# Cross attention with another order of one step's turns on TensorE, ScalarE and VectorE, and squares taken from SBUF

## What is computed

```python
kvx = jnp.einsum('bsi,oi->bso', cond, w_kv_x)
kx, vx = jnp.split(kvx, 2, axis=-1)
kx = _ln(kx.reshape(b, sc, g, d), kxln_w, kxln_b)
vx = vx.reshape(b, sc, g, d)
xout = _gqa(qx, kx, vx).reshape(b, s, nh * d)
...
cat = jnp.concatenate([core, xout], axis=-1)
catq = _div_clamp_fp8(cat, proj_smooth)
```

## Time and profile before

| | us |
|---|---|
| median of 3 runs | 2798.78 (2798.61 to 2798.89) |
| the profiled execution | 2799.96 |
| its span | 2798.2 |
| PE busy, share of the span | 2278.0 (81%) |
| DVE | 2104.4 (75%) |
| POOL | 1571.4 (56%) |
| ACT | 1554.5 (56%) |
| DMA queue 1, share of the 16 engines' span | 12.3% |

### The profile page before, as it was taken

How to read it: one execution, slowest core, us unless ns; L and a number is a source line. 1 busy time by engine, 2 the same in 40 slices (tenths; PEclk the granted TensorE clock), 3 DMA queues, 4 the chain that set the end, 5 groups by cost and what they waited for, 6 DMA issues and landing times. The chain is left out here.

```text
span 2798.2 us, 50477 instructions
## 1 busy us (share of the span) xinstructions
PE 2278.0 (81%) x18514; PEld 1812.5 (65%) x18514; DVE 2104.4 (75%) x4502; ACT 1554.5 (56%) x3129; POOL 1571.4 (56%) x1619
## 2 busy tenths in 40 slices
PE   2466662699999999999999999999999999855556
PEld 1243441578877877877877877877877878644334
DVE  8888885477787778778787787778778787558763
ACT  4455451566666666666666666666666667411211
POOL 2465655766766766767666766766767655340000
PEclk8687875999999999999999999999999999977778
DMA  2001103110010010110110111010010100073100
GB/s 105 16 29 40 46 23 115 55 38 31 26 50 32 25 44 34 31 44 32 32 38 31 34 43 32 32 44 26 31 52 25 32 9 1 1 271 96 40 12 8
DMA packets 74482, 119.45 MB, mean 43 GB/s; under 512 B 21168, under 2 KB 56576, under 8 KB 73216
## 3 DMA queue, kind: packets, MB, share of 16 engines
q1 hardware_dynamic: 74240, 116.23, 12.3%
HBM read 94.20 MB, written 22.02 MB: 42 GB/s over the span
## 5 line engine op out<-in xcount | busy, mean ns | idle before, releaser
L71 PE MATMUL x_kc<-x_wk,x_ctxT 128*128 128x256 f16 x4992 | 622.8, 274 | 52.8 <-POOL x_ctxT L975 40.0
L997 POOL TENSOR_TENSOR x_kT<-x_kf,x_kT 128x512 f16<-128x512 f32 (+1 forms) x448 | 629.6, 1405 | 37.3
L71 PE MATMUL x_ox<-x_ctxp,x_pt 128*128 128x256 f16 x4992 | 619.0, 273 | 0.0
L995 POOL TENSOR_SCALAR x_kT<-x_kf 128x512 f16<-128x512 f32 (+1 forms) x448 | 288.2, 643 | 583.8 <-ACT x_kf L1067 581.8
L71 PEld LDWEIGHTS x_kc<-x_wk,x_ctxT 128*128 128x128 f16 x4992 | 481.6, 98 | 131.6 <-issue 40.2
L71 PEld LDWEIGHTS x_ox<-x_ctxp,x_pt 128*128 128x128 f16 x4992 | 486.3, 98 | 70.1 <-DVE x_on L1328 14.0
L1055 ACT ACTIVATE x_kraw<-x_kc 128x512 f32<-128x512 f32 (+1 forms) x448 | 254.3, 568 | 426.3 <-PE x_kc L71 214.5
L1263 DVE TENSOR_REDUCE x_ss<-x_sq 128x4 f32<-128x512 f32 (+1 forms) x448 | 283.1, 642 | 230.5 <-ACT x_sq L1059 228.9
L1320 DVE TENSOR_TENSOR x_pt<-x_tp,x_pt 128x512 f16<-128x512 f32 (+1 forms) x512 | 297.4, 584 | 117.5 <-ACT x_pt L1094 113.7
L1067 ACT ACTIVATE x_kf<-x_tp,x_hv 128x512 f32<-128x512 f32 (+1 forms) x448 | 330.7, 755 | 76.5 <-PE x_tp L1146 72.7
L1181 PE MATMUL x_tp<-x_ident,x_pb 128*128 128x128 f32 x1664 | 256.5, 274 | 52.8 <-ACT x_pb L1088 50.6
(11 more groups left out here) (234 smaller groups left out, 3181.5 us busy)
## 6 DMA issues: line engine op xcount, KB each, us to landing
x_stage<-in_ctxT SPq DMA_DIRECT2D x32, 800.5 KB, 4.3
x_stage<-in_ctx SPq DMA_DIRECT2D x16, 896.0 KB, 5.1
x_stage<-in_ctx SPq DMA_DIRECT2D x16, 640.0 KB
scr_q<-a_qxT SPq DMA_DIRECT2D x8, 1024.0 KB, 3.9
x_qs<-scr_q SPq DMA_DIRECT2D x16, 512.0 KB, 5.4
scr_core<-a_catc SPq DMA_DIRECT2D x8, 512.0 KB, 2.6
scr_x<-x_catx SPq DMA_DIRECT2D x8, 512.0 KB, 2.6
f_area<-in_wprojT SPq DMA_DIRECT2D x4, 1024.0 KB, 11.4
```

The costliest lines, as they stand in the source:

```text
L71: last = pe.matmul(out, lhs[i], rhs[j], start=start and n == 0, stop=stop and n == len(parts) - 1)
L995: gp.tensor_scalar(dst[0], src, 1.0, 0.0, ALU.mult, ALU.add).then_inc(khi_ready, 1)
L997: gp.tensor_tensor(dst[1], src, dst[0], ALU.subtract).then_inc(kT_ready, 1)
```

## The change

The three lists of order are changed. On PE the third `pv` stands where `m` 1 stood and `m` 1 comes after `ob`; both first turns of probabilities follow it, then `tr` 2 and `m` 2; the last `pv` comes before `pt` 0 2. ACT follows that order, with `tr` ahead of `m` for units 1 and 2. On DVE `ob` comes ahead of the sums `m` 0 and `m` 1, `on` of the second group ahead of `pt` 0 2, and most `rs` move behind `pt` 1 1. The square is read from `kraw` in SBUF in place of the PSUM bank `kc`, so ACT waits for its own copy first, and PE's next `m` waits for the copy, no longer for the square.

```diff
--- before.py
+++ after.py
@@ -800,21 +800,21 @@
 
 
 
-        ORDER = [("m", 0), ("sr", 0), ("sc", 0), ("pv", -1, 0), ("pv", -1, 1), ("tr", 0), ("oa", -2), ("m", 1),
-                 ("tr", 1), ("ob", -2), ("pt", 0, 0), ("pv", -1, 2), ("pt", 0, 1), ("m", 2), ("tr", 2), ("pt", 0, 2),
-                 ("pv", -1, 3), ("pt", 0, 3), ("m", 3), ("tr", 3), ("sr", 1), ("sc", 1), ("m", 4), ("pv", 0, 0),
+        ORDER = [("m", 0), ("sr", 0), ("sc", 0), ("pv", -1, 0), ("pv", -1, 1), ("tr", 0), ("oa", -2), ("pv", -1, 2),
+                 ("tr", 1), ("ob", -2), ("m", 1), ("pt", 0, 0), ("pt", 0, 1), ("tr", 2), ("m", 2), ("pv", -1, 3),
+                 ("pt", 0, 2), ("pt", 0, 3), ("m", 3), ("tr", 3), ("sr", 1), ("sc", 1), ("m", 4), ("pv", 0, 0),
                  ("tr", 4), ("oa", -1), ("pv", 0, 1), ("m", 5), ("tr", 5), ("ob", -1), ("tr", 6), ("pv", 0, 2),
                  ("pt", 1, 0), ("m", 6), ("pt", 1, 1), ("pt", 1, 2), ("pv", 0, 3), ("pt", 1, 3)]
 
-        ACT_ORDER = [("sr", 0), ("m", 0), ("tr", 0), ("oa", -2), ("exp", 0), ("m", 1), ("tr", 1), ("pt", 0, 0),
-                     ("pt", 0, 1), ("m", 2), ("tr", 2), ("pt", 0, 2), ("pt", 0, 3), ("m", 3), ("tr", 3), ("sr", 1),
+        ACT_ORDER = [("sr", 0), ("m", 0), ("tr", 0), ("oa", -2), ("exp", 0), ("tr", 1), ("m", 1), ("pt", 0, 0),
+                     ("pt", 0, 1), ("tr", 2), ("m", 2), ("pt", 0, 2), ("pt", 0, 3), ("m", 3), ("tr", 3), ("sr", 1),
                      ("m", 4), ("tr", 4), ("oa", -1), ("exp", 1), ("m", 5), ("tr", 5), ("tr", 6), ("pt", 1, 0),
                      ("m", 6), ("pt", 1, 1), ("pt", 1, 2), ("pt", 1, 3)]
-        DVE_ORDER = [("norm", 0), ("max", 0), ("oa", -2), ("norm", 1), ("m", 0), ("m", 1), ("ob", -2), ("quant", 0),
-                     ("pt", 0, 0), ("pt", 0, 1), ("quant", 1), ("m", 2), ("pt", 0, 2), ("on", -1), ("pt", 0, 3),
+        DVE_ORDER = [("norm", 0), ("max", 0), ("oa", -2), ("norm", 1), ("ob", -2), ("m", 0), ("m", 1), ("quant", 0),
+                     ("pt", 0, 0), ("pt", 0, 1), ("quant", 1), ("m", 2), ("on", -1), ("pt", 0, 2), ("pt", 0, 3),
                      ("quant", 2), ("m", 3), ("max", 1), ("quant", 3), ("m", 4), ("oa", -1), ("m", 5), ("quant", 4),
-                     ("ob", -1), ("pt", 1, 0), ("m", 6), ("rs", 0), ("rs", 1), ("rs", 2), ("pt", 1, 1), ("rs", 3),
-                     ("rs", 4), ("pt", 1, 2), ("rs", 5), ("rs", 6), ("on", 0), ("rs", 7), ("rs", 8), ("pt", 1, 3),
+                     ("ob", -1), ("pt", 1, 0), ("m", 6), ("pt", 1, 1), ("rs", 0), ("rs", 1), ("rs", 2), ("rs", 3),
+                     ("pt", 1, 2), ("rs", 4), ("on", 0), ("rs", 5), ("rs", 6), ("rs", 7), ("rs", 8), ("pt", 1, 3),
                      ("rs", 9), ("rs", 10)]
         TP_KINDS = ("sr", "tr", "pt", "oa", "ob")
         TP_STEP = [o for o in ORDER if o[0] in TP_KINDS]
@@ -1056,7 +1056,9 @@
                                ).then_inc(kraw_ready, 1)
                 if not (isinstance(JK, int) and u < 2):
                     act.wait_ge(ss_ready, u - 1)
-                act.activation(sq[:, (jk * KU + i) % 2, 0:n], src, ACT.Square).then_inc(sq_ready, 1)
+                act.wait_ge(kraw_ready, 4 + u + 1)
+                act.activation(sq[:, (jk * KU + i) % 2, 0:n], kraw[:, 4 * i:4 * i + n // P, :].rearrange("p n d -> p (n d)"),
+                               ACT.Square).then_inc(sq_ready, 1)
 
             def keep_k(JK, jk, i, bank):
                 u = JK * KU + i
@@ -1127,7 +1129,7 @@
 
                     pe.wait_ge(ctxT_ready, 8 * (JK // SPB + 1) if isinstance(JK, int) else JK * 2 + 8)
                 if not (isinstance(JK, int) and u < 1):
-                    pe.wait_ge(sq_ready, u)
+                    pe.wait_ge(kraw_ready, 4 + u)
                 gp_ = jk % SPB
                 slot = (jk // SPB) % 2
                 for n, c in enumerate(chunks(i)):
```

## The result

The changed kernel takes 2826.34 us, median of 4 runs (2825.90 to 2829.08), against 2798.82 for the kernel before: a ratio of 1.010, 95% interval 1.0083 to 1.0118. It is 27.5 us slower. The execution profiled took 2825.90 us, its span 2824.1. The prediction said 2815, slower, with 2778 to 2836 as its range.

What follows compares the result with a forecast made beforehand. The prediction took PE's work plus its gaps as the bound in cross attention. 43 steps at 0.34 + 0.17 gave +22, `quant` steps 0, four other steps +1, setup -6: +17, median 2815 us, range 2778 to 2836.

Steps and rivals of the forecast that it cites:

- The 0.79 us wait: PE's wait at `pt` 0 0 for ACT's exponentials in every step: it goes, by itself worth 46 us.
- The chain to `sr` 1: First half of a step, ACT's copies through DVE's sum, `on` and `pt` 0 2: `sr` 1 at 15.42, 0.34 later.
- The price of the hold: DVE's `rl` addition, held until POOL's instruction ends: 0.4 us each step; unheld, `sr` 1 at 15.05 and 2799 in all.
- The sign that was named for it: DVE's `rl` addition in the new trace: still near 0.95 us in half of its calls.
- Squares from SBUF: ACT's square after its copy: distance 0.63 where it was 0.49; second half 0.17 longer where POOL waited for `kf` 5.
- the end plus 0.03: ACT's square of the copy: assumed to start 0.03 us after the copy's end, as DVE's dependent pairs do.
- `rs` and `sr` 0: End of a step: POOL releases `sr` 0, 0.14 us behind it, so moving DVE's `rs` behind `pt` 1 1 gives nothing.
- The `quant` step: The 14 steps with `quant`, bounded by POOL: `sr` 1 near 16.2, 0 change taken, range -1.0 to +0.5 each.
- The setup: The 14 units made before the steps: PE's waits for the square shrink, about -6 us.
- The six other steps at the two ends: Steps outside the 43 and the 14: +1 us for four of them, the last two unchanged.
- The rival named "worse": DVE's tail holds exp 0 by 0.3 per step and the `quant` step pays 0.5: 2838 us, chance 0.15.
- The faster rival: Squares right behind copies, `rl` ahead of POOL's instruction: `sr` 1 at 14.84, -0.24 in 43 steps, 2771 us, chance 0.20.

Runs made afterwards that it cites:

- experiment 5: Changed kernel with squares read from PSUM again and `on` back behind `pt` 0 2 on DVE: 2750.93 us, ratio 0.9819 to the kernel before.
- experiment 1: Changed kernel with `on` of the second group put back behind `pt` 0 2 on DVE: 2768.79 us, ratio 0.9879 to the kernel before.
- experiment 2: Changed kernel with squares read from PSUM and PE waiting for the square again, `on` left ahead: 2813.01 us, ratio 1.0039 to the kernel before.
- experiment 7: Changed kernel with the `rl` addition written as tensor_scalar, its second input read as a scalar: 2819.56 us, ratio 1.0061 to the kernel before.
- experiment 4: Kernel before with only DVE's `rs` moved behind `pt` 1 1 and 1 2: 2802.88 us, ratio 1.0001 to the kernel before.
- experiment 6: Kernel of experiment 5 with ACT working `tr` 5 (`kf` 5) ahead of `m` 5: 2744.51 us, ratio 0.9797 to the kernel before.
- 8: Changed kernel with PE waiting for the square again only in the 14 units before the steps: 2832.90 us, ratio 1.0113 to the kernel before.
- 9: Kernel before with only `on` of the second group moved ahead of `pt` 0 2 on DVE: 2809.91 us, ratio 1.0041 to the kernel before.
- 10: Kernel of experiment 5 with DVE's `ob` again behind the sums of `m` 0 and `m` 1: 2832.56 us, ratio 1.0122 to the kernel before.
- 3: Kernel before with only the squares read from the copy in SBUF, order lists untouched: 2831.38 us, ratio 1.0102 to the kernel before.

## Why the prediction was right, and where its sizes were off

**The sign and the mechanism held.** The 0.79 us wait went. Behind it `sr` 1 got later by DVE's chain and `sr` 0 by ACT's. By itself the new order is worth 0.62 in the first half of a third step and 51 us in all (experiment 5), where 46 was said for the wait. Experiments 1 and 2 take the two costs away one at a time and 5 together. Without `on` ahead the first half recovers, with squares from PSUM the second half does; the first half does not recover with the squares alone.

**The chain to `sr` 1** was foreseen link by link, in us after `sr` 0: copy of `m` 2 at 11.70 (measured 1454.59 - 1442.85 = 11.74), its sum at 13.0 (13.10), `rl` standing at 13.6 (13.70) and ending at 14.0 (13.99), `pt` 0 2 at 14.67 (14.63), `sr` 1 at 15.42 (15.37).

**The price of the hold was read wrongly from this chain, though its end was right.** The prediction said that `sr` 1 would come at 15.05 were `rl` not held, and made 2799 of that. Experiment 7 has 15.28 and 2819.56. Two small misses did it: ACT's chain came 0.1 later, so that `rl` met only the last 0.29 of POOL's instruction, and of that it would have taken 0.15 unheld, which the 15.05 left out. What costs is all of `on` in front of `pt` 0 2, 0.93 us by starts, of which the form of `rl` is a tenth (0.09). The sign that was named for it failed too: `rl` was to take near 0.95 us in half of its calls, and in that half it takes 0.29 or 0.30 in most steps and 0.52 in the `quant` step. In the third step it stands 0.88 behind the start of POOL's instruction, where it stood 0.23 behind it. The Trainium skill (SBUF — State Buffer, section SBUF: two separate sides) has VectorE, in an instruction with two SBUF inputs, and GpSimd block each other for whole instructions; the trace agrees in that `rl` ended within 0.02 of POOL's instruction in the earlier trace rows, after the change and in experiment 2. It did not tell which of the two chains sets the end, and the prediction leaned on it too heavily: it was one of two almost equal limits, ACT's chain being the other. Experiment 2 shows the other case, where the hold is binding.

**Squares from SBUF.** The distance copy to square was foreseen at 0.63 and is 0.69. The step that failed is "the end plus 0.03": ACT's dependent pair starts 0.09 after the copy's end (1454.59 + 0.60 = 1455.19, square 1455.28). The square itself takes 0.63, as taken. The second half grew by 0.23 in the third step, where +0.17 was said; the first by 0.29, where +0.34 was said. The sum, 0.52, is the +0.51 of the forecast, but that close by luck: one half was put too high and the other too low.

**`rs` and `sr` 0.** Nothing was foreseen, nothing came in all (experiment 4), for the reason given: POOL stood 0.14 ahead. Experiment 6 shows the whole chain `m` 5, `kf` 5, POOL, `sr` 0: taking `m` 5 out of it shortened the second half by 0.50.

**The `quant` step** is the term that was mis-sized. `sr` 1 near 16.2 and no change in all was said; it is 15.88 and +0.33. Its first half grew by 0.80, its second shrank by 0.47. Fourteen such steps are +4.6 us. The prediction let POOL's earlier start and the later `sr` 1 cancel. By the experiments (means of `quant` steps) the new order is worth -1.12 (5), `on` ahead then costs 1.17 (2 against 5), and the squares 0.28 (2 against the change): the first two do nearly cancel, and the third, the price of the squares, is what was left out.

**The setup** was foreseen at -6 and is -3.4, of which 1.5 lie ahead of the first unit, where nothing was edited; from the first unit on it is -1.9. The waits shrank as said; a lower clock took most of it, as the section on the hardware shows. The six other steps at the two ends cost some 3 us where 1 was said.

Against the span: 43 x 0.51 = +22 (said +22), `quant` +4.6 (said 0), setup -3.4 (said -6), the other steps +3.2 (said +1), what follows -0.5 (said 0), in all +25.9 (said +17), with rounding. The rival named "worse" was not what happened, though its 2838 is as near to the result as the forecast's 2815: DVE's tail does not hold exp 0, which in the third step starts at t = 1449.08 - 1442.85 = 6.23, exactly as before.

**The faster rival** (2771) did not come about. Experiment 1 lies near its number (2768.79), by luck: there the third step has -0.63 in the first half and +0.24 in the second, where the rival had -0.24 and 0. The rival said that it decides whether `pt` 0 2 starts before or after t = 14.33, and this point was well chosen: 13.71 in experiment 1, 14.63 in the change. The squares did not need to be any faster for it, only `on` had to be elsewhere.

## What to carry to other kernels

An edit that removes a wait on the bounding engine also removes the idle time that covered other work: `on` ahead of `pt` 0 2 cost 0.21 a step while DVE waited for ACT there and 0.92 once it did not, so the bundle is 1% slower than before, and the same bundle without that one entry 1.2% faster. When a row names one engine as the releaser of a wait and another engine ended 0.14 us before the wait did (experiment 4), count both as releasers, and price only what removes both. A pass that reads another engine's bank looks free to move to SBUF, but ask what its new dependence on the copy costs on the engine that makes both, and whose chain that engine's next instruction starts.

## What the runs showed of the hardware

**TensorE's clock before the steps.** 14 units are made there in two loops of seven, each full unit by 12 matmuls. Two units of the changed kernel, one of each loop, in PE's order of time:

```profile
501.33 2.74 PE L71 MATMUL x_kc<-x_wk,x_ctxT 128*128 128x256 f16 x12 [0.69 <-ACT x_kraw L1055]
...
518.39 1.48 PE L71 MATMUL x_kc<-x_wk,x_ctxT 128*128 128x256 f16 x12 [0.25 <-ACT x_kraw L1055]
```

The first took 2.74 us, where it was 1.48 before. Busy time by stretch, 493 to 512 us, of the kernel before and of the changed one:

```profile
493.00:512.00 19.00, 6.76 (x54) 4.87 (x54) 9.35 (x18) 5.42 (x11) 16.29 (x23) 0.85 0.46 136
```

```profile
493.00:512.00 19.00, 10.50 (x47) 5.97 (x45) 7.14 (x18) 5.71 (x10) 14.73 (x21) 0.50 0.42 138
```

The granted clock is 0.50 in the changed kernel, the lower level of 1.2 GHz. A unit takes 2.74 + 0.69 = 3.43 us there, by starts, and 2.66 before the change. In the second loop, at the full clock, it is 2.17, the 0.49 less that was foreseen.

In all eight kernels in which PE waits for the square there (before, 2, 4, 5, 6, 8, 9, 10) the full clock came with the second or third unit of the first loop. Of the four in which it does not (the changed one, 1, 3, 7), three stayed at the lower level up to the end of that loop. The fourth, experiment 7, whose edit touches nothing before the steps, had the full clock from its second unit on:

```profile
489.48 1.49 PE L71 MATMUL x_kc<-x_wk,x_ctxT 128*128 128x256 f16 x12 [0.69 <-ACT x_kraw L1055]
...
498.18 0.83 PE L71 MATMUL x_kc<-x_wk,x_ctxT 128*128 128x256 f16 x6 [0.69 <-ACT x_kraw L1055]
```

Its last unit of the first loop starts at 498.18 in place of 504.76, its second loop at 508.12 in place of 512.87, and its first `sr` 0 stands at 525.21 in place of 529.86. From the first unit (483.84, 484.12 after the change, 485.60 before) to the first `sr` 0 are 41.37 us in experiment 7, 45.74 after the change and 47.67 before: a gain of 6.3 us at the full clock, the 6 that were predicted, and of 1.9 at the lower one. So the lower clock cost 4.4 us. That one execution of experiment 7 took 2814.85 us and its other three 2819.5 to 2820.6, which would fit the same 4.4 us, but they were not profiled. Each kernel has one profiled execution. Why PE with shorter pauses is mostly granted less here stays open.

**ScalarE's pairs.** A copy from PSUM and an independent square of the same bank stand 0.49 apart; a square of the copy stands 0.68 to 0.71 behind it in the full units of the steps, with 0.09 between the copy's end and the square's start, and takes 0.63 in place of 0.59 to 0.61.

**A one-column instruction can take two to six times its shortest time.** The addition of two columns on VectorE took 0.15 us with POOL idle, and 0.29 after the change, 0.70 in experiment 2 and 0.95 before beside POOL's 1.16 us instruction with two SBUF inputs; written with its second input as a scalar it took 0.20 in all 99 cases of experiment 7, in the same place.
